# Drawing the lead-in of one self-attention stage apart and setting unread matmuls around it

## The reference, cut to what matters

```python
x_norm = modulate(_ln(x), shift_a, scale_a)
qkv = x_norm @ W_qkv + b_qkv
q, k, v = jnp.split(qkv, 3, axis=-1)          # then (B, 16 heads, 1024, 16)
attn_w = jax.nn.softmax(jnp.einsum('bhqd,bhkd->bhqk', q, k) * scale, axis=-1)
attn_out = jnp.einsum('bhqk,bhkd->bqhd', attn_w, v)
x = x + gate_a[:, None] * (attn_out @ W_proj + b_proj)
```

## Time and profile before

| | |
|---|---|
| time, three runs | 1666.86 us median (1666.84 to 1670.57) |
| the profiled execution | 1668.83 us, of which the span of its instructions is 1666.8 us |
| PE busy | 1526.9 us (92%) |
| DVE busy | 1048.8 us (63%) |
| ACT busy | 769.6 us (46%) |
| POOL busy | 379.3 us (23%) |
| mean granted TensorE clock | 0.969 of full speed |

### The profile page before, as it was taken

How to read it: one execution, slowest core, us unless ns; L and a number is a source line. 1 busy time by engine, 2 the same in 40 slices (tenths; PEclk the granted TensorE clock), 3 DMA queues, 4 the chain that set the end, 5 groups by cost and what they waited for, 6 DMA issues and landing times.

```text
span 1666.8 us, 26374 instructions
## 1 busy us (share of the span) xinstructions
PE 1526.9 (92%) x10485; PEld 926.8 (56%) x10485; DVE 1048.8 (63%) x2946; ACT 769.6 (46%) x1228; POOL 379.3 (23%) x419
## 2 busy tenths in 40 slices
PE   5899998999998999878998999899999899987898
PEld 3447674444354857556764767444444475655676
DVE  3573344999627445899357334499982734579953
ACT  1334421688843533325443443148885354333444
POOL 3510006342016010114133000434400701001320
PEclk9899999999999999999999899999999999999999
DMA  9400017221020000000130000632202000000000
GB/s 336 143 1 0 0 41 147 36 40 26 2 76 1 1 1 3 1 1 1 56 109 1 0 1 0 161 49 40 40 2 77 1 1 1 3 1 1 1 1 26
DMA packets 37551, 59.60 MB, mean 36 GB/s; under 512 B 7360, under 2 KB 26980, under 8 KB 36532
## 3 DMA queue, kind: packets, MB, share of 16 engines
q1 hardware_dynamic: 25239, 34.71, 6.3%
q0 software_dynamic: 9408, 15.85, 6.2%
q10 hardware_dynamic: 2780, 7.36, 1.3%
HBM read 42.03 MB, written 2.10 MB: 26 GB/s over the span
## 4 chain that ended last, share of the span: by engine, by line
PE 68%; DVE 19%; issue 6%; ACT 4%; DMA 1%; POOL 1%; ACTq 0%; DVEq 0%; POOLq 0%
PE ps L993 9%; PE ps L1005 8%; PE ps L464 7%; PE ps L1299 4%; PE ps L978 3%; PE ps L870 3%; PE ps L1092 3%; DVE taken L2351 3%; PE ps L1100 3%; DVE rs L2036 2%; PE ps L848 2%; PE ps L592 2%; DVE mxw L2028 2%; PE ps L600 2%; PE ps L1156 2%
## 5 line engine op out<-in xcount | busy, mean ns | idle before, releaser
L2221 DVE TENSOR_REDUCE mm<-ps 128x1 f32<-128x1024 f32 x256 | 310.1, 1222 | 32.8 <-PE ps L978 25.6
L1618 ACT ACTIVATE pt<-ps 128x512 f32<-128x512 f32 x512 | 276.7, 600 | 59.1 <-PE ps L993 42.4
L2464 POOL TENSOR_TENSOR rstd<-ve,minus_half 128x4 f32<-128x4 f32 x32 | 35.7, 1114 | 745.0 <-DVE ve L1900 745.0
L993 PE MATMUL ps<-qx,kx 64*128 64x512 f32 x512 | 188.3, 445 | 1.0 <-ACT pt L1618 1.0
L978 PE MATMUL ps<-kx,qx 48*128 48x512 f32 x512 | 186.6, 444 | 0.2
L1005 PE MATMUL ps<-pt,v 128*32 128x256 f32 x2048 | 158.7, 390 | 0.0
L993 PEld LDWEIGHTS ps<-qx,kx 64*128 64x128 f32 x512 | 79.0, 184 | 95.9 <-ACT pt L1618 85.9
L2111 DVE TENSOR_TENSOR rlo<-ring,rhi 128x512 fp32r<-128x512 f32 x48 | 33.2, 692 | 121.6 <-ACT ring L1568 121.5
L1005 PEld LDWEIGHTS ps<-pt,v 128*32 128x32 f32 x2048 | 42.9, 108 | 85.5 <-ACT pt L1618 60.4
L978 PEld LDWEIGHTS ps<-kx,qx 48*128 48x128 f32 x512 | 75.4, 184 | 22.0 <-issue 18.0
L592 PE MATMUL ps<-filler 128*128 128x512 f32 x262 | 83.6, 434 | 0.0
(11 more groups left out here) (373 smaller groups left out, 3397.5 us busy)
## 6 DMA issues: line engine op xcount, KB each, us to landing
wm<-in_L_xcond_W_mlp_dram SPq DMA_DIRECT2D x4, 1024.0 KB, 8.3
qx<-q_hi POOLq DMA_DIRECT2D x64, 64.0 KB, 2.6
kx<-k_hi POOLq DMA_DIRECT2D x64, 64.0 KB, 2.8
w3a<-in_L_xcond_w_m_dram SPq DMA_DIRECT2D x2, 2048.0 KB, 8.2
w<-in_L_xcond_e_w_dram SPq DMA_DIRECT2D x6, 512.0 KB, 6.9
w<-in_L_xcond_e_w_dram SPq DMA_DIRECT2D x2, 1536.0 KB, 13.6
s_ada<-in_L_xcond_w_ada_dram ACTq DMA_DIRECT2D x1, 2304.0 KB, 24.3
qx<-q_lo POOLq DMA_DIRECT2D x32, 64.0 KB, 2.6
```

Source lines behind the costliest of these rows:

```text
L993: pe.matmul(ps[:, bank, :], kx[r, p % 4, kc * P:(kc + 1) * P], qx[r, p % 4, half * 512:(half + 1) * 512], start=True, stop=True).then_inc( ...
L1618: act.activation(pt[:, u % 8, half * 512:(half + 1) * 512], ps[:, bank, :], ACT.Exp, scale=QK_SCALE).then_inc(st_read, 1)
L2221: return dve.tensor_reduce(mm[:, p % 2, e, t:t + 1], place(), X, ALU.max).then_inc(ring_read, 1)
```

## The change

The change touches only the lead-in of this stage. PE reports the products of block 0 as they are done, sets nine unread matmuls before the turning of block 1 and four after it, starts q of block 1 on the first half of `hT`, makes only four of the eight full matmuls (`full_step`) and seven unread matmuls ahead of the first unit, the other four behind units 0 to 3, and the gates' three behind unit 7. The unread pairs ahead of units begin with the sixth unit. ACT and DVE make high and low parts in halves of 512 columns, those of block 0 ahead of block 1's `hT`. POOL waits for each part of spread 0 by itself, and issues the parts of a spread in the order q_hi, q_lo, k_hi, k_lo.

```diff
                 values(0)
                 routed_out(1)
-                linear(0, wqk2, 0, hT[:, 0])
+                linear(0, wqk2, 0, hT[:, 0]).then_inc(full_done, 1)
                 residual(1, 1)
                 pe.wait_ge(v_ready, b * NB + 1)
-                linear(2, wqk2, KC, hT[:, 0])
+                linear(2, wqk2, KC, hT[:, 0]).then_inc(full_done, 1)
+                keep_busy(6, 9)
                 ln(2, 1)
+                keep_busy(6, 4)
...
+                def full_step(j):
+
+                    qk, k, c = j // 4, j // 2 % 2, j % 2
+                    ins = pe.matmul(ps[:, 4 + 2 * qk + k, :], wqk2[:, c, (qk * KC + 1) * P:(qk * KC + 2) * P], hT[:, k, c, :], start=c == 0, stop=c == KC - 1)
+                    if j == 7:
+                        ins.then_inc(full_done, 1)
...
-                pe.wait_ge(hT_ready, b * 2 * N_HT + 12)
-                for qk in range(2):
-                    queries_keys(0, qk, take(), (1,)).then_inc(ring_ready, 1)
+                linear(take() + 1, wqk2, 0, hT[:, 1], (hT_ready, b * 2 * N_HT + 10)).then_inc(ring_ready, 1)
+                linear(take() + 1, wqk2, KC, hT[:, 1]).then_inc(ring_ready, 1)
                 values(1)
-                queries_keys(1, 0, 4)
+                for j in range(4):
+                    full_step(j)
+                pe.wait_ge(v2_clear, b + 1)
                 pe.wait_ge(v_ready, b * NB + NB)
-                queries_keys(1, 1, 6).then_inc(full_done, 1)
-                pe.wait_ge(v2_clear, b + 1)
-                pe.wait_ge(ring_read, b * N_RING + 2)
-                keep_busy(2, 9)
-                pe.wait_ge(full_ready, b + 1)
-                for j in range(3):
...
+                keep_busy(6, 7)
...
-                    if n < 4:
-                        keep_busy(7, 2 if n < 0 else 1)
+                    if m == 5:
+                        pe.wait_ge(full_ready, b * 2 + 1)
+                    if m >= 5 and n < 4:
+                        keep_busy(4 if m < 2 * T else 7, 2 if n < 0 else 1)
                     if m < UNITS:
...
                         query_scores(q, at_m)
+                    if m < 4:
+                        full_step(m + 4)
+                    elif m == 7:
+                        pe.wait_ge(full_ready, b * 2 + 2)
+                        for j in range(3):
...
+                def high_part(qk, k):
+
+                    col = (C_BQ2, C_BK2)[qk]
+                    affine(dense[2 * qk][:, k * BLK:(k + 1) * BLK], ps[:, 2 * qk + k, :], 1.0, colT[:, col:col + 1]).then_inc(hi_ready, 1)
+
+                for qk in range(2):
+                    act.wait_ge(full_done, b * 3 + qk + 1)
+                    high_part(qk, 0)
+                ln(2, 1, (mod, M_SC_A, M_SH_A))
...
                 for qk in range(2):
-                    high_parts(0, qk)
-                act.wait_ge(full_done, b + 1)
+                    act.wait_ge(ring_ready, u0 + qk + 1)
+                    high_part(qk, 1)
+                act.wait_ge(full_done, b * 3 + 3)
...
                 for qk in range(2):
-                    low_parts(qk)
+                    low_part(qk, 0)
+                for qk in range(2):
+                    place()
+                    low_part(qk, 1).then_inc(ring_read, 1)
...
+                        for part in range(2):
+                            if p == 0:
+                                if part == 0:
+                                    pool.wait_ge(hi_ready, b * 6 + 2 + qk + 1)
+                                else:
+                                    pool.wait_ge(ring_read, b * N_RING + qk + 1)
+                                pool.sem_inc(passed, 1)
```

More of the change, by code:

```diff
@@ L1016, in finish @@
                     ins.then_inc(ring_ready, 1)
-                pe.wait_ge(hT_ready, b * 2 * N_HT + 12)
-                for qk in range(2):
-                    queries_keys(0, qk, take(), (1,)).then_inc(ring_ready, 1)
+                linear(take() + 1, wqk2, 0, hT[:, 1], (hT_ready, b * 2 * N_HT + 10)).then_inc(ring_ready, 1)
+                linear(take() + 1, wqk2, KC, hT[:, 1]).then_inc(ring_ready, 1)
                 values(1)
-                queries_keys(1, 0, 4)
+                for j in range(4):
+                    full_step(j)
+                pe.wait_ge(v2_clear, b + 1)
                 pe.wait_ge(v_ready, b * NB + NB)
-                queries_keys(1, 1, 6).then_inc(full_done, 1)
-                pe.wait_ge(v2_clear, b + 1)
-                pe.wait_ge(ring_read, b * N_RING + 2)
-                keep_busy(2, 9)
-                pe.wait_ge(full_ready, b + 1)
-                for j in range(3):
-                    o = N_ROW * b + R_G_A + j
-                    ins = pe.matmul(ps[:, 5 + j // 2, j % 2 * D:(j % 2 + 1) * D], row_of[:, o:o + 1].broadcast_to([64, P]), row_hl[:, :], start=True, stop=True)
-                ins.then_inc(gates_spread, 1)
+                keep_busy(6, 7)
                 for n in range(-LEAD, UNITS):
@@ L1049, in _ @@
                         query_scores(q, at_m)
+                    if m < 4:
[3 more added lines that the diff above has]
+                        for j in range(3):
+                            o = N_ROW * b + R_G_A + j
+                            ins = pe.matmul(ps[:, 5 + j // 2, j % 2 * D:(j % 2 + 1) * D], row_of[:, o:o + 1].broadcast_to([64, P]), row_hl[:, :], start=True, stop=True)
+                        ins.then_inc(gates_spread, 1)
                     if n >= 0:
@@ L1586, in _ @@
                         ln(2, 0, (mod, M_SC_A, M_SH_A), 2)
-                ln(2, 1, (mod, M_SC_A, M_SH_A))
                 u0 = b * N_RING
                 keys, turned = [0], {}
[L1593 to L1600, removed]
+                def high_part(qk, k):
[5 more added lines that the diff above has]
+                ln(2, 1, (mod, M_SC_A, M_SH_A))
                 def next_key():
@@ L1626, in _ @@
                 for qk in range(2):
-                    high_parts(0, qk)
-                act.wait_ge(full_done, b + 1)
+                    act.wait_ge(ring_ready, u0 + qk + 1)
+                    high_part(qk, 1)
+                act.wait_ge(full_done, b * 3 + 3)
                 for qk in range(2):
                     col = (C_BQ2, C_BK2)[qk] + 1
-                    ins = affine(full[qk], ps[:, 4 + 2 * qk:6 + 2 * qk, :].rearrange("p a q -> p (a q)"), 1.0, colT[:, col:col + 1])
-                ins.then_inc(full_ready, 1)
+                    affine(full[qk], ps[:, 4 + 2 * qk:6 + 2 * qk, :].rearrange("p a q -> p (a q)"), 1.0, colT[:, col:col + 1]).then_inc(full_ready, 1)
                 act.wait_ge(gates_spread, b + 1)
@@ L1635, in _ @@
                 act.activation(gates[:, 2, :], ps[:, 6, 0:D], ACT.Copy).then_inc(gates_ready, 1)
-                act.wait_ge(full_ready, b + 1)
+                act.wait_ge(full_ready, b * 2 + 2)
                 for i in range(4):
@@ L1639, in _ @@
                 for qk in range(2):
-                    high_parts(1, qk)
+                    act.activation(dense[2 * qk][:, :], full[qk], ACT.Copy).then_inc(hi_ready, 1)
                 scored = 2
@@ L2211, in place, with low_part @@
                     return ps[:, 2 * (n % 2):2 * (n % 2) + 2, :].rearrange("p a q -> p (a q)")
[L2213 to L2217, removed]
+                def low_part(qk, k):
+                    dve.wait_ge(hi_ready, b * 6 + 2 * k + qk + 1)
+                    col, r = (C_BQ2, C_BK2)[qk], slice(k * BLK, (k + 1) * BLK)
+                    return dve.scalar_tensor_tensor(dense[2 * qk + 1][:, r], ps[:, 2 * qk + k, :], colT[:, col:col + 1], dense[2 * qk][:, r].bitcast(F32),
+                                                    ALU.add, ALU.subtract)
                 def query_maximum(p, u):
@@ L2486, in spread @@
                 def spread(p):
-                    if p == 0:
-                        pool.wait_ge(ring_read, b * N_RING + 2)
                     if p == NP // 2:
@@ L2493, in spread @@
                         pool.wait_ge(st_ready, b * N_KEY + 4 * T * (p - 3) + p - 2)
-                    if p == 0 or p >= 4:
                         pool.sem_inc(passed, 1)
                     for qk, wide in enumerate((qx, kx)):
[L2497 to L2500, removed]
+                        for part in range(2):
[5 more added lines that the diff above has]
+                                pool.sem_inc(passed, 1)
+                            for e in range(2):
+                                r = 32 * (p % 4) + HD * e
+                                for i in range(3):
+                                    if ((0, 1, 0), (0, 0, 1))[qk][i] == part:
+                                        pool.dma_start(wide[64 * e + HD * i:64 * e + HD * (i + 1), p % 4, :], dense[2 * qk + part][r:r + HD, :]).then_inc(spread_ld[p % 4], 16)
                 def maximum_rows(p):
@@ L2529, in _ @@
                         for qk in range(2):
-                            pool.wait_ge(hi_ready, b * 2 * KC + 2 + qk + 1)
+                            pool.wait_ge(hi_ready, b * 6 + 4 + qk + 1)
```

## The result

The changed kernel takes 1695.59 us (median of four runs, 1692.11 to 1700.09) against 1666.85 us before (1660.26 to 1670.57): a ratio of 1.0179, 95% interval 1.0158 to 1.0201. The forecast was 1654.3 us, faster.

A forecast was written before the change was run, and what follows sets the result against it. It took PE to bound the kernel, with DVE setting the steady self-attention; an earlier first unit gains 6.4 us in entry 0 and 6.2 in entry 1, 12.6 in all, from 1666.86 to 1654.3 us, range 1650.0 to 1661.5.

The forecast's parts named there:

- Clock at the turning: Behind block 1's turning, unread matmuls keep the clock full, so q and k take 3.42 us in place of 6.33.
- POOL: In spread 0, POOL's first issue comes 6.8 us sooner (260.2 against 266.98) and its three later waits cost zero.
- First unit: The first self-attention unit starts at 269.2 in place of 277.61, 8.4 us sooner.
- Units 0 to 3: Each carries a full matmul of 0.86 us in place of the unread pair's 0.66, losing 0.8 us in all.
- The wait ahead of unit 5: PE waits for ACT's first full copy until 276.5; unit 5 then starts at 277.2, leaving 7.0 us of gain.
- The rival that ended slower: Behind the lead-in, half-clock stretches fall otherwise; 35 us more at half speed would give 1671.8 us; chance 0.07.
- its last sign: The prediction is wrong if the gain at unit 8 (6.4 us) is no longer there at the end.
- The sum: Gains of 6.4 us in entry 0 and 6.2 in entry 1, 12.6 in all, bring the median to 1654.3 us.
- What is late next: ACT's high parts of half 1 end at 294.2, turned maxima come at 294.4; PE gain above about 7 us is cut.

The follow-up runs named there:

- e8: e1 without the nine and the four unread matmuls around the turning of block 1; 1658.08 us (one run).
- e1: The changed kernel with unread pairs ahead of units 5, 6 and 7 put into the unit's own ps banks, so PE skips the wait for ACT's copy; 1644.91 us.
- e7: The changed kernel with ACT's copy of q's full product in two halves, unit 5's unread pair waiting for the first half only; 1649.37 us.
- e9: The changed kernel with four unread matmuls in place of two ahead of units 8 to 21; 1690.62 us (one run).
- e3: The changed kernel with 16 unread matmuls more ahead of unit 10; 1670.24 us (one run).
- e5: The change's front alone, all full matmuls ahead of the first unit, pairs ahead of every unit, plus one 1.32 us pause ahead of unit 5's pair; 1707.41 us.

## Why the prediction was wrong

Its terms, counted from the turning in entry 0:

- *Clock at the turning:* right. Two linears took 3.54 us, forecast 3.42, and the clock was 1.00 from 249.2 to 255.0. e8 shows that the unread matmuls on the two sides of the turning, taken together, did it. The sentence on transposes in the Trainium skill ("TensorE: Matmul & The Clock Gate", Part 4) is not contradicted: in e8 a bare turning, behind 3.14 us of idle time, went with a fall to 0.50, and with unread matmuls on both sides there was none.
- *POOL:* the first issue came 5.6 us behind the turning in place of 12.5, 6.9 sooner (forecast 6.8), and the three later waits cost nothing but 0.1:

POOL in the changed kernel, the first spread, to be laid beside the earlier trace rows:

```profile
254.84 2.05 POOL L2514 DMA_DIRECT2D qx<-q_hi  x4 [5.82 <-ACT q_hi L1418]
256.87 0.98 POOL L2514 DMA_DIRECT2D qx<-q_lo  x2
257.94 1.92 POOL L2514 DMA_DIRECT2D kx<-k_hi  x4
259.85 0.97 POOL L2514 DMA_DIRECT2D kx<-k_lo  x2
```

- *First unit:* 8.8 us sooner, forecast 8.4.
- *Units 0 to 3:* mis-sized a little. A unit with a full matmul takes 1.71 us ((270.49 - 263.63) / 4), not 1.52: between scores the full matmul took 1.06 us (264.29 to 265.35), where 0.86 had been reckoned from a run of its kind.
- *The wait ahead of unit 5:* here the prediction failed, in the step "PE waits for it ahead of unit 5's pair until 276.5". The wait was there and of the length forecast (0.55 us against 0.6, from 275.3 and unit 4's 0.66 to 276.5). It was priced at its own length, and what the clock does behind it was put at nothing without a reason: the sum went on with pairs of 0.66 us, as if the clock, weighed with care at the turning, were settled for the rest of the lead-in. What the runs showed in its place is that this wait costs the clock, for 54 us in entry 0 (without it, in e1, the clock stays at 1.00): from unit 5 to the mark behind the units the changed kernel takes 23.1 us longer than before in entry 0 and 21.6 in entry 1, against 6.6 and 6.4 gained by then.
- *The rival that ended slower* had the right quantity and the wrong place. It looked for more half-clock time all over the kernel behind the lead-in, with "35 us more" for 1671.8 and a chance of 0.07; it was 90 us more (193 - 103), and the two stretches behind the pauses, from 274 to 328 and from 1089.8 to past 1140, more than make that up. The prediction's own list of what would prove it wrong looks at the clock between 256 and 263 only; its last sign, a gain at unit 8 that is gone at the end, came about.
- *The sum:* with the pause gone (e1), the marks behind the units come 6.1 and 6.5 us sooner than before, 12.6 in all. That this is the forecast's sum is in part luck: the first unit came 0.4 us sooner than reckoned, units 0 to 3 lost 0.8 more, and e1 lacks the 0.6 us of the wait. In entry 0 the gain was 6.8 us at unit 16; part of it went in 0.39 us of waiting for the maxima rows ahead of the first key-side place (PE of e1 at 294.81), the limit that the prediction had named under "What is late next". The median fell by 20 us. In the two profiled executions, 22.9 us apart, the 10.3 that are not the stage's lie mostly ahead of the first turning (it starts at 249.50 us in e1, at 254.44 before) and behind the second entry's units (385.2 us to the end in place of 389.7), at mean clocks of 0.97 in place of 0.95 and 0.96. But for the nine unread matmuls and two short copies in the idle time ahead of the turning the program is the same there, and in e7, which is the same up to that point as e1, the first turning starts at 252.49; no run ties these 10.3 us to the change.

## What to carry to other kernels

Where unread matmuls are there to hold TensorE's clock, price a wait twice: by its length, and by what the clock does behind it. Ask at every place of a lead-in whether the work behind the wait could raise the clock again by itself; if not, half a microsecond may cost tens: between e1 and the changed kernel 0.55 us made a difference of 22.6 and 21.7 us at the mark behind the units. Waits of unread work are the cheapest to remove, since nobody reads what it writes: put into the bank that the next real matmul will overwrite, it waits only for what that matmul has to wait for anyway.

## What the runs showed of the hardware that was not expected

- A half-speed stretch can last while PE's records leave no gap: 43.00 of 43.00 us busy at 0.50 in e9, 54 of 54 in the changed kernel. The Trainium skill says on the page "TensorE: Matmul & The Clock Gate" (Part 1, "What's actually happening") that "activity releases the throttle". e3's run of 18 unread matmuls agrees with it; these stretches do not, if busy time is taken as activity.
- The same list of pairs and scores held 1.00 where it was reached at 1.00 (e1 from 276 to 290 us, e3 from 289 to 310) and stayed at 0.50 where it was reached at 0.50 (the changed kernel from 274 us).
- Idle time of PE among the units, and what followed: 0.12 us (e7, 274.62 - 273.77 - 0.73) no fall in two entries, 0.55 us a fall in five of six (the changed kernel, e3, e9), 1.32 us a fall in two of two (e5, whose units all have their pairs).
